# Cross-attention and a 4-bit feed-forward on one core: the first batch's order of work, where its k chunks land, and when the packed weights are unpacked

## The reference, cut to what matters

```
xn  = layernorm(x);  q = Wq·xn, k = Wk·ctx, v = Wv·ctx          (8 heads of 64, HIDDEN 512)
q   = softmax over a head's 64 rows * scale;  k = softmax over the 1024 columns
out = Wo·((k·vT)T·q) + bo;  x = x + out / norm(out) * g * sqrt(128)
y   = layernorm(x)·w + bias;  x = x + y      w: 1024x1024, unpacked from qweight (512x1024 int32,
                                             a low and a high nibble each), zero points, scales
```

## Time and profile before

| | us |
|---|---|
| median of three runs (lowest, highest) | 633.75 (632.51, 635.59) |
| the profiled execution's own time, its span | 635.1, 633.3 |
| busy of the span: PE, PEld | 596.1, 380.6 |
| busy of the span: DVE, ACT, POOL | 543.2, 507.1, 548.9 |

### The profile page before, as it was taken

How to read it: one execution, slowest core, us unless ns; L and a number is a source line. 1 busy time by engine, 2 the same in 40 slices (tenths; PEclk the granted TensorE clock), 3 DMA queues, 4 the chain that set the end, 5 groups by cost and what they waited for, 6 DMA issues and landing times.

```text
span 633.3 us, 10844 instructions
## 1 busy us (share of the span) xinstructions
PE 596.1 (94%) x3431; PEld 380.6 (60%) x3447; DVE 543.2 (86%) x904; ACT 507.1 (80%) x789; POOL 548.9 (87%) x473
## 2 busy tenths in 40 slices
PE   4686799999999999999999999999999999998897
PEld 3454375656657575665657566665756666574654
DVE  4897789898988999888988988898898989889754
ACT  4888789797879879787988979797897978788442
POOL 4268879999999999999999999999899999999630
PEclk9888799999999999999999999999999999999999
DMA  9416658868596876868887885868698595848551
GB/s 324 108 36 147 120 140 152 208 97 208 116 151 184 157 189 129 187 125 171 167 138 184 142 202 117 179 143 141 182 152 198 121 194 116 154 116 162 111 141 67
DMA packets 246969, 96.19 MB, mean 152 GB/s; under 512 B 236136, under 2 KB 237952, under 8 KB 246912
## 3 DMA queue, kind: packets, MB, share of 16 engines
q1 hardware_dynamic: 240576, 72.42, 59.3%
q10 hardware_dynamic: 6336, 23.07, 10.7%
HBM read 28.85 MB, written 8.39 MB: 59 GB/s over the span
## 4 chain that ended last, share of the span: by engine, by line
PE 74%; DVE 9%; ACT 5%; issue 4%; DMA 3%; POOL 3%; SPq 1%; ACTq 0%; POOLq 0%; DVEq 0%
PE ps_m L1619 14%; PE ps_m L1493 7%; PE ps_k L1411 4%; PE ps_o L1503 4%; PE ps_o L1411 4%; PE ps_o L1412 4%; PE ps_o L1413 4%; PE ps_k L1413 4%; PE ps_k L1412 4%; PE ps_q L1411 3%; PE ps_q L1413 3%; PE ps_q L1412 3%; PE ps_ta L1472 2%; PE ps_o L1527 2%; PE ps_tb L1472 2%
## 5 line engine op out<-in xcount | busy, mean ns | idle before, releaser
L514 POOL TENSOR_TENSOR q_tok_lo<-q_exp,q_tok_hi 128x1024 f16<-128x1024 f32 x64 | 135.8, 2132 | 8.1 <-ACT q_tok_hi L748 7.3
L737 ACT ACTIVATE q_exp<-q_exp,w_unit 128x512 f32<-128x512 f32 x128 | 92.9, 726 | 53.4 <-DVE q_exp L1070 53.3
L486 POOL TENSOR_TENSOR q_exp<-q_exp,q_rec 128x1024 f32<-128x1024 f32 x63 | 119.9, 1904 | 4.9
L1065 DVE TENSOR_REDUCE q_nmax<-ps_q 128x8 f32<-128x512 f32 x128 | 86.9, 679 | 28.5 <-PE ps_q L1413 28.2
L1619 PE MATMUL ps_m<-w_int,x_parts 128*128 128x512 f16 x432 | 100.0, 379 | 0.3 <-DMA x_parts<-spare 0.2
L1070 DVE TENSOR_TENSOR q_exp<-ps_q,q_nmax 128x512 f32<-128x512 f32 x128 | 88.5, 692 | 4.4
L522 POOL TENSOR_TENSOR k_lo<-k_exp,k_hi 128x1024 f16<-128x1024 f32 x32 | 82.2, 2569 | 9.2 <-ACT k_hi L678 9.2
L1056 DVE TENSOR_REDUCE k_nmax<-ps_k 128x1 f32<-128x1024 f32 x64 | 77.1, 1205 | 5.2 <-PE ps_k L1413 4.9
L1493 PE MATMUL ps_m<-k_t,c_t 128*128 128x256 f32 x256 | 77.0, 383 | 0.0
L1077 DVE TENSOR_REDUCE q_sum<-q_exp 128x16 f32<-128x1024 f32 x64 | 76.9, 1201 | 0.0
L748 ACT ACTIVATE q_tok_hi<-q_exp 128x1024 f16<-128x1024 f32 x64 | 67.5, 1054 | 7.8 <-POOL q_exp L486 5.4
(11 more groups left out here) (221 smaller groups left out, 1461.7 us busy)
## 6 DMA issues: line engine op xcount, KB each, us to landing
x_res<-in_x ACTq DMA_DIRECT2D x16, 512.0 KB, 3.6
out_x<-y SPq DMA_DIRECT2D x15, 512.0 KB, 2.9
x_in<-in_x ACTq DMA_DIRECT2D x14, 512.0 KB, 4.8
c_in<-in_ctx ACTq DMA_DIRECT2D x14, 512.0 KB, 6.0
x_in<-in_x SPq DMA_DIRECT2D x2, 512.0 KB, 5.6
c_in<-in_ctx SPq DMA_DIRECT2D x2, 512.0 KB, 7.0
q_hi<-q_tok_hi SPq DMA_TRANSPOSE x64, 3.3
q_lo<-q_tok_lo SPq DMA_TRANSPOSE x64, 3.3
```

The costliest lines, as they stand in the source:

```text
L486: nc.gpsimd.tensor_tensor(pair, pair, rec.unsqueeze(2).to_broadcast([P, 2 * HEADS, DH]), ALU.mult).then_inc(qs_done, 1)
L514: nc.gpsimd.tensor_tensor(q_tok_lo[p % 2][:], q_exp[:, 2 * p:2 * p + 2, :].rearrange("p t d -> p (t d)"), q_tok_hi[p % 2][:], ALU.subtract ...
L737: nc.scalar.activation(q_exp[:, j, :], q_exp[:, j, :], ACT.Exp, scale=w_unit[:]).then_inc(qexp_done, 1)
L1065: nc.vector.tensor_reduce(q_nmax[:, j, :], heads, op=ALU.max, axis=AX_X, negate=True).then_inc(qmax_done, 1)
```

## The change

Three things are done, all in the stages -1, 0 and 1. **Banks:** ps_o becomes one two-bank tile, and batch 0's chunks 1 and 3 go there instead of into ps_k, so chunk 1 needs no wait for chunk 0's exponential, chunk 2 waits for that of chunk 0, and chunk 3 for that of chunk 1. vo is made in the same banks, now after all four chunks and their transposes; Wv, Wo and the turned Wo move to rows 5 to 7 of q_exp. Exponential and high part of chunk 1 go into stage -1 on ACT, ahead of the second half of the turned context. **M:** the spread of vo's magnitudes goes to ps_ta instead of ps_m; `mix_m` of batch 0 no longer waits for `vtop_done`, the next batch's `transpose_c` does; on PE four token tiles of M come before q chunk 4 and the other four before q chunk 5, and the next batch's chunk 0 before q chunk 6. `move_m` comes before `high_q(0)` on ACT. **Nibbles:** tiles 2 and 3 are picked in stage 1, after `shift_q(0)` and `shift_q(1)`, into the places that tiles 0 and 1 used, and converted in stage 1; the q_lo transposes lose their wait. The order of stage 0 on ACT, DVE and PE is rewritten. The diff, without the lines that only rename buffers:

```diff
-        q_lo_flat = q_lo[:].rearrange("p t c r -> p (t c r)").bitcast(I32)
         q_low = [y[:].bitcast(I32), x2_parts[:].rearrange("p a t c -> p (a t c)").bitcast(I32),
-                 q_lo_flat[:, 0:OUT], q_lo_flat[:, OUT:2 * OUT]]
+                 y[:].bitcast(I32), x2_parts[:].rearrange("p a t c -> p (a t c)").bitcast(I32)]
...
-        ps_o = [psum(f"ps_o{h}", [P, BANK]) for h in range(2)]
+        ps_oo = psum("ps_o", [P, HALVES * BANK])
+        ps_o = [ps_oo[:, h * BANK:(h + 1) * BANK] for h in range(2)]
...
+        def k_bank(b, j):
+            return ps_oo if b == 0 and j % 2 == 1 else ps_k
...
@@ SP, turn_q
-                elif name == "lo":
-                    sp.wait_ge(w_converted, 2 * RC)
@@ ACT, stage -1
                     move_tc(0)
-                    exp_k(n, 1 - s, 0)
+                    for j in range(TURNED):
+                        exp_k(n, 1 - s, j)
+                        high_k(n, j)
                     move_tc(1)
-                    high_k(n, 0)
@@ ACT, stage 0
                 if i == 0:
+                    exp_k(a, s, 2)
                     exp_q(0)
-                    exp_k(a, s, 1)
+                    exp_k(a, s, 3)
+                    move_tk(0)
+                    exp_q(1)
+                    for k in range(1, TK):
+                        move_tk(k)
                     move_vo()
-                    high_k(a, 1)
-                    exp_q(1)
-                    exp_k(a, s, 2)
+                    part_rows(0)
+                    high_c()
                     convert_nibble(0, 0)
                     exp_q(2)
                     convert_nibble(0, 1)
-                    exp_k(a, s, 3)
-                    move_tk(0)
-                    move_tk(1)
-                    part_rows(0)
-                    high_c()
-                    move_tk(2)
-                    move_tk(3)
+                    exp_q(3)
                     convert_nibble(1, 0)
-                    exp_q(3)
+                    part_rows(1)
                     convert_nibble(1, 1)
-                    part_rows(1)
                     exp_q(4)
-                    convert_nibble(2, 0)
-                    convert_nibble(2, 1)
                     exp_q(5)
+                    move_m(a)
                     high_q(a, 0)
-                    convert_nibble(3, 0)
-                    convert_nibble(3, 1)
                     exp_q(6)
                     high_q(a, 1)
                     exp_q(7)
                     high_x()
-                    move_m(a)
                     norm_x()
@@ ACT, stage 1: convert_nibble(2, 0) after exp_q(1), (2, 1) after high_c, (3, 0) and (3, 1) after exp_q(4)
@@ DVE
-                nc.vector.tensor_reduce(v_top[:], ps_m[:, 0:P], op=ALU.max, axis=AX_X).then_inc(vtop_done, 1)
+                nc.vector.tensor_reduce(v_top[:], ps_ta[:, 0:P], op=ALU.max, axis=AX_X).then_inc(vtop_done, 1)
...
+                if m >= 2:
+                    dve.wait_ge(w_converted, 4)
...
-                    if i == 0 and j == 2:
+                    if i == 0 and j == 5:
                         dve.wait_ge(vo_ready, 1)
@@ DVE, stage 0
                     shift_q(0)
-                    set_up_rows()
                     max_k(a, 1)
+                    max_k(a, 2)
                     low_tc(a, s, 1)
                     shift_q(1)
+                    max_k(a, 3)
+                    set_up_rows()
+                    shift_q(2)
                     pick_nibbles(0)
-                    max_k(a, 2)
-                    shift_q(2)
+                    shift_q(3)
                     pick_nibbles(1)
-                    max_k(a, 3)
-                    pick_nibbles(2)
-                    pick_nibbles(3)
-                    shift_q(3)
                     set_up_gains()
                     shift_q(4)
+                    sum_q(a, 0)
                     set_up_top()
-                    sum_q(a, 0)
                     invert_k()
                     shift_q(5)
                     abs_c()
@@ DVE, stage 1
                 shift_q(0)
                 if i > 1:
                     split_g(c)
+                else:
+                    pick_nibbles(2)
                 max_k(a, 2)
                 low_tc(a, s, 1)
                 if do_f:
                     low_x2(f)
                 shift_q(1)
+                if i == 1:
+                    pick_nibbles(3)
                 max_k(a, 3)
@@ PE
+                pe.wait_ge(kexp_done, HC)                       (set_up_vo)
...
+                pe.wait_ge(tk_moved, TK - 1)                    (set_up_spread)
-                nc.tensor.transpose(ps_m[:, 0:P], v_abs[:].to_broadcast([P, P]), ident[:]).then_inc(vabs_ready, 1)
+                nc.tensor.transpose(ps_ta[:, 0:P], v_abs[:].to_broadcast([P, P]), ident[:]).then_inc(vabs_ready, 1)
...
-                    if begun(4 * b + j):                        (project_k)
+                    if b > 0:
                         pe.wait_ge(kexp_done, 4 * b + j)
+                    elif j == 1:
+                        pe.wait_ge(ctop_done, 1)
+                    elif j > 1:
+                        pe.wait_ge(kexp_done, j - 1)
...
+                        if i == 0:                              (transpose_c)
+                            pe.wait_ge(vtop_done, 1)
...
-                        if i == 0:                              (mix_m)
-                            pe.wait_ge(vtop_done, 1)
@@ PE, stage 0
                     project_k(a, 1)
-                    set_up_vo()
+                    project_k(a, 2)
                     project_q(1)
-                    project_k(a, 2)
-                    project_q(2)
                     project_k(a, 3)
                     transpose_k(0)
                     transpose_k(1)
-                    project_q(3)
+                    project_q(2)
                     transpose_k(2)
                     transpose_k(3)
+                    set_up_vo()
+                    project_q(3)
+                    mix_m(0, 4)
                     project_q(4)
                     set_up_spread()
+                    mix_m(4, TC)
                     project_q(5)
-                    mix_m(0, 4)
-                    project_q(6)
                     transpose_c(0)
                     spread_c()
-                    mix_m(4, 6)
+                    project_k(n, 0)
+                    project_q(6)
+                    mix_g(a)
                     project_q(7)
-                    mix_m(6, TC)
-                    project_k(n, 0)
                     transpose_c(1)
-                    mix_g(a)
                     project_k(n, 1)
```

More of the change, by code:

```diff
@@ L189, in build @@
         wk_in = k_flat[:, HID:2 * HID].rearrange("p (k c) -> p k c", k=HC)
-        wv_in = k_flat[:, 2 * HID:3 * HID].rearrange("p (k c) -> p k c", k=HC)
-        wo_in = k_flat[:, 3 * HID:4 * HID]
-        wo_t = k_flat[:, 4 * HID:5 * HID].rearrange("p (k o) -> p k o", k=HC)
+        wv_in = k_flat[:, 5 * HID:6 * HID].rearrange("p (k c) -> p k c", k=HC)
+        wo_in = k_flat[:, 6 * HID:7 * HID]
+        wo_t = k_flat[:, 7 * HID:8 * HID].rearrange("p (k o) -> p k o", k=HC)
         ps_q = psum("ps_q", [P, BANK])
@@ L669, in exp_k @@
                             act.wait_ge(tk_ready, TK * of + 2 * (held - TURNED) + 2)
-                    nc.scalar.activation(k_exp[:, j % 2, :], ps_k[:], ACT.Exp, bias=bias,
+                    nc.scalar.activation(k_exp[:, j % 2, :], k_bank(b, j)[:], ACT.Exp, bias=bias,
                                          accum_out=k_sum[:, sums, j:j + 1]).then_inc(kexp_done, 1)
@@ L951, in iteration @@
                 exp_q(1)
+                if i == 1:
+                    convert_nibble(2, 0)
                 high_q(c, 3)
@@ L960, in iteration @@
                     high_c()
+                if i == 1:
+                    convert_nibble(2, 1)
                 squares(0)
@@ L966, in iteration @@
                 exp_q(4)
+                if i == 1:
+                    convert_nibble(3, 0)
+                    convert_nibble(3, 1)
                 exp_q(5)
@@ L1055, in max_k @@
                         dve.wait_ge(kbias_done, TURNED * (b - 1) + j + 1)
-                    nc.vector.tensor_reduce(k_nmax[:, j:j + 1], ps_k[:], op=ALU.max, axis=AX_X,
+                    nc.vector.tensor_reduce(k_nmax[:, j:j + 1], k_bank(b, j)[:], op=ALU.max, axis=AX_X,
                                             negate=True).then_inc(kmax_done, 1)
@@ L1395, in set_up_vo @@
                 pe.wait_ge(ctop_done, 1)
+                pe.wait_ge(kexp_done, HC)
                 for h in range(HEADS):
@@ L1404, in set_up_spread @@
                 pe.wait_ge(vabs_done, 1)
-                nc.tensor.transpose(ps_m[:, 0:P], v_abs[:].to_broadcast([P, P]), ident[:]).then_inc(vabs_ready, 1)
+                pe.wait_ge(tk_moved, TK - 1)
+                nc.tensor.transpose(ps_ta[:, 0:P], v_abs[:].to_broadcast([P, P]), ident[:]).then_inc(vabs_ready, 1)
             def iteration(i, s, do_n, do_a, do_c, do_f):
```

(12 more changed lines are left out.)

## The result

The changed kernel takes 644.9 us in the median of six runs (642.53 to 646.84), the kernel before 633.9 on the same chip: ratio 1.017 (1.014 to 1.020). It is slower, as forecast, but by 11.0 us and not by 5.0, and lies above the range. It was run again on two more occasions, on two chips: 1.0109 (1.005 to 1.0168) and 1.013 (1.0095 to 1.0165). The first profiled execution took 643.27 us, span 641.5, against 635.1 and 633.3.

What follows compares the result with a forecast made beforehand. PE bounds the kernel from stage 2 on; in stages 0 and 1 PE and DVE wait in turns, and delays there move the end. Stage 0's 1.6 plus stage 1's 3.4 made +5.0 on median 633.75: 638.8 us, range 632.0 to 641.5.

Steps and rivals of the forecast that it cites:

- Banks: Batch 0's chunks: chunk 1 starts on PE about 14.6, chunk 3's maximum on DVE at 24.3 instead of 29.05.
- rival 4: The banks do nothing for the end, as M's tiles eat the lead; already in the sum, no chance of its own.
- The collisions: Nibbles of tiles 1 to 3 meet POOL in stages 0 and 1, POOL's instruction between a pair's halves; chance 0.60.
- rival 1: Stages 0 and 1: POOL waits, nibble pairs run through whole once started; 634.5 us, chance 0.16.
- Rival 2: Stages 0 and 1: nibbles and POOL don't meet at all, nibbles stay hidden; 633.4 us, chance 0.12.
- Rival 3: No collision, and earlier picks end stage 1's half-clock stretch; 630.5 us, chance 0.12.
- Stage 0: +1.6: Collision at tile 1 makes batch 1's first exponential 1.6 us late; half clock on M's tiles 4 to 7 excluded.
- 0.9 lost and 0.57 won: Stage 0 behind q5's shift: q6's shift comes 0.9 us later, `move_m` leaving ACT's tail wins 0.57.
- +3.4: Stage 1: squares of batch 0's second output half wait for q5's exponential and come 3.4 us late.
- Pair 2: Tile 2's nibbles in stage 1 meet POOL's scaling and `low_k`; chunk 2's maximum 3.5 us late.
- Released during DVE's previous instruction, POOL goes next: Order rule for stages 0 and 1: POOL takes its turn between a pair's nibbles, up to 2.36 us.
- Pair 3: Tile 3's nibbles in stage 1 have 2.13 us of POOL between halves; chunk 3's maximum +5.3 in all.

Runs made afterwards that it cites:

- the reductions' 0.63: Kernel before with the nibble part alone, each stage 1 nibble of tiles 2 and 3 replaced by a maximum over 512 columns: 635.03 us.
- after: The changed kernel itself, first measurement: 644.9 us, ratio 1.017 to the kernel before.
- after_again: The changed kernel, unaltered, measured again for comparison with other versions on the same chip: 641.95 us.
- after_third: The changed kernel, unaltered, measured a third time beside other versions on the same chip: 643.18 us.
- warm_less: The changed kernel plus dummy matmuls, results unread, in PE's idle stretches of stages 0 and 1: 645.23 us.
- pick1_early: The changed kernel with tile 1's nibbles unpacked ahead of q3's shift in stage 0, not behind it: 638.39 us when first timed.
- pairs_late: As pick1_early, with tiles 2 and 3 unpacked in stage 1 behind q3's shift, ahead of a sum POOL waits on: ratio 1.0118 to the kernel before.

## Why the prediction was wrong

**Banks: right.** Less the start's 1.24 us, chunk 1 starts at 14.4 (forecast 14.6) and chunk 3's maximum at 24.3 (24.3). The lead is eaten, as rival 4 in the sum had it.

**The collisions: there in all three places,** in all three traces of the changed kernel, and in two of them as forecast: at tiles 1 and 3 one nibble of the pair is stretched by 1.8 to 2.0 us. At tile 2 the first nibble waits for POOL's scaling (1.64), as forecast, but then the pair runs through and POOL waits, which is rival 1's order (below). So rival 1 falls for two places of three. Rival 2 falls, and the reductions' 0.63 excludes that any DVE work stretches there. Rival 3 falls: the clock fell more, not less.

**The step that failed: "Stage 0: +1.6", with the half clock left to the upper end.** The forecast is of batch 1's first exponential. It starts 4.3, 3.3 and 3.9 us late in after, after_again and after_third (57.37, 54.97 and 56.67 for 51.79, less the start's shift). The rows of after_again and after_third:

```profile
54.97 1.11 ACT L672 ACTIVATE k_exp<-ps_k,k_bias 128x1024 f32<-128x1024 f32 x1
```

```profile
56.67 1.11 ACT L672 ACTIVATE k_exp<-ps_k,k_bias 128x1024 f32<-128x1024 f32 x1
```

At q5's shift the three are +4.8, +3.7 and +4.3, where +2.1 was forecast. In the first trace that is 2.1 as forecast, 1.4 for two tiles of M at half clock (1.49 and 1.45, 0.76 at full), and 1.4 for vo and the transposes ahead of it, also at half clock: vo ended at 32.63, or 31.4 by the old start, where 30.0 was forecast. after_again has vo at full clock, ending at 30.2 by the old start, and the tiles at half. after_third has vo (2.08) and q3 (1.26 for 0.65) at half clock and tiles 4 to 7 at full:

```profile
30.52 2.08 PE L1406 MATMUL ps_o<-q_exp 64*128 64x128 f32 x16
32.53 0.61 PE L1420 MATMUL ps_q<-wq_hi,xn_lo 128*128 128x512 f16 x1
```

Each trace has one or the other, the first both, so the term belonged in the sum, about 2 us of it (1.6 to 2.7). The forecast counted it for tiles 4 to 7 alone and put vo and q3 at nothing. Behind q5's shift 0.4 us are won in each trace (forecast 0.5). But the terms that the prediction names for that, 0.9 lost and 0.57 won, make 0.3 lost: in the first trace q6 loses 1.0 and `move_m` wins 0.6, and that ACT comes to `high_x` 0.6 sooner behind q7's shift, and is 0.3 quicker from there, was not in the forecast.

**Stage 1: near +3.4 only by other terms.** From the first exponential to the squares of the second output half the three traces lose 3.5, 2.1 and 1.8. Batch 1's chunk 1 at half clock, behind the 5.89 us of waiting, had been put at nothing and costs 1.3 in all three (0.0 in warm_less, at full clock). Pair 2 costs 0.95 at chunk 2's maximum (forecast 3.5): tile 2's second nibble got in ahead of `low_k` (0.70), and POOL waited (2.49 for 2.13). "Released during DVE's previous instruction, POOL goes next" holds where it is released early enough: `low_k` at 67.94 came after that nibble had begun. Pair 3 costs 1.4 at chunk 3's maximum (forecast 1.8; its nibble took 2.51). The second output half is reached 3.5, 3.3 and 2.5 late (forecast 3.8; the terms given for it, 5.3 less 1.0, make 4.3). It then runs in part at half clock in the first trace (0.69), as before, and at full clock in the other two, which is what they gain. The squares wait for q5's exponential, as forecast, in after_third only.

**The sum and the median.** From the same start the three traces end +7.0, +4.0 and +4.2 us later: +5.0 stands among them, by errors of opposite sign. That is luck, and not a sum that was right. The second step that failed is that I added it to a median. The first comparison is 633.75, + 1.35 (the profiled execution of before above its median), + 1.24 (later start), + 7.0, + 1.63 (the median after above its profiled execution) = 645.0, measured 644.9. In two of the three comparisons the profiled execution was the quickest of the changed kernel's six. By mean clock, medians of all timed executions (one of 1577 us left out):

```
clock             0.979-0.981   0.984-0.987   0.989-0.992   0.995-1.000
before (114)       639.5 (13)    635.8 (29)    634.7 (45)    632.7 (24)
after (18)         643.9 (13)    642.1 (5)
pick1_early (33)   641.7 (16)    637.0 (13)
```

Each row's missing executions are under 0.978. At like clock the changed kernel is 4.4 to 6.3 us slower, near the forecast; the rest, by this table, is that 13 of its 18 executions lie in the first column and 13 of 114 before. This is a grouping and not a test, since an execution's mean clock itself follows from its waits, and warm_less had the clock without the time. The traces show half clock behind the changed kernel's longer waits in stage 0 (2.31 us ahead of the spread, in both traces that have it; 2.12 ahead of chunk 3's transposes, in two of three), but not behind every long wait: behind the 2.83 us ahead of 17.56 the kernel before is at full clock. The timed executions have no trace, so that their waits bring the clock down more often is inferred.

## What to carry to other kernels

Put VectorE's elementwise work on SBUF tiles where GpSimd is bound to rest, not where VectorE happens to wait: a wait filled beside GpSimd costs the waits of all who hang on it, here 4 us for 2, and a change of clock or order can move it under the next instruction. Where a change gathers TensorE's waits into fewer, longer ones in a stage that isn't full, the half-clock term belongs in the sum. A difference worked out in one profiled execution is the median's only if the change leaves the scatter as it was.

## What the runs showed that I had not expected

The same code ran with different parts at half clock: pick1_early's stage 0 was at 1.00 from 28.9 to 32.6 and from 33.2 to 40.0 us, while pairs_late, the same up to there, had its vo at 1.87 us and batch 1's chunk 0 at half clock, 4 us of difference at batch 1's first maximum:

```profile
30.71 1.87 PE L1409 MATMUL ps_o<-q_exp 64*128 64x128 f32 x16
...
44.37 0.32 PE L1478 MATMUL ps_o<-ident,c_abs 128*128 128x128 f32 x1 [2.20 <-DVE c_abs L1211]
44.47 0.62 PE L1423 MATMUL ps_k<-c_hi,wk_lo 128*128 128x512 f32 x1
```

And the first loads' landing moves the start by up to 2.2 us (first maximum at 14.62 to 16.83), whatever the kernel.
